# Relative-key products of the diagonal tile: whole-width products against strips of 32 keys

## The chip, the cores and the metric

The kernel runs on one core of one Trainium2 chip. The metric is device time in microseconds (us) of one launch. The engines: PE is TensorE (PEld its weight loads), ACT is ScalarE, DVE is VectorE, POOL is GpSimd, SP only issues DMAs.

## The reference, cut to what matters

Batch 16, sequence 512, model width 128, 16 heads of 8 elements. A layer norm, then attention with relative positions clipped to 20 on either side, then a residual, a second layer norm and a gated feed-forward part of width 384.

```python
idx = jnp.clip(pos[None, :] - pos[:, None], -20, 20) + 20     # (query, key) -> 0..40
rk2, rv2 = rel_k[idx], rel_v[idx]
attn1 = jnp.einsum('bhqd,bhkd->bhqk', q, k)
attn2 = jnp.einsum('bhqd,qkd->bhqk', q, rk2)
attn = softmax((attn1 + attn2) / sqrt(8))
w1 = jnp.einsum('bhqk,bhkd->bhqd', attn, v)
w2 = jnp.einsum('bhqk,qkd->bhqd', attn, rv2)
x = x + (w1 + w2) @ Wo.T + bo
x = x + (silu(ln(x) @ wg.T) * (ln(x) @ wu.T)) @ wd.T
```

What matters here is `attn2`: for a query q only the keys within 20 of it (the band) have a relative row of their own. All keys further below share `rel_k[0]`, all keys further above share `rel_k[40]`.

## The kernel before, in words

There are three stages, one after the other: a projection stage over 16 batches, an attention stage, and an output stage over 16 batches.

**Units and pairs.** The attention stage takes units: one batch and one tile of 128 queries, 64 units in all. Two units of a batch form a pair (32 pairs). Scores are made transposed: keys on the partitions, (head, query) on the columns, in PSUM banks of 512 columns. There are three such banks (`b_s`, NBANK = 3), used in turn. Each pair has 16 chunks, each chunk fills two banks; ACT takes the exponential of each bank (L1111) into `b_p`.

**Chunks of a pair** (`CHUNK`, L602): chunks 0 and 1 are the first unit's diagonal tile (keys and queries of one tile), 2 and 3 its neighbour tile, 4 and 5 another tile; 6 and 7 belong to the second unit's tile at position 0, 8 and 9 are the second unit's diagonal tile, 10 and 11 its tile at position 2, and 12 to 15 the last tile for both units. So there are four diagonal chunks in a pair, 128 in the kernel.

**A diagonal chunk before.** For each of its two banks (n = 0, 1), `scores` (L916) waits for the bank (`wait_bank`), ahead of bank 0 issues the row products of a later unit (`row_pairs_ahead`, L845, two products side by side), then `diagonal_scores` (L909): 8 products of 118 rows by 128 keys on 64 columns (two heads by 32 queries), and then `relative_scores` (L894): 16 products, one for each block of QB = 2 queries, with the 128 keys' weights cut out of the table `z` and 32 columns (16 heads by 2 queries) of the expanded query `qd`. The last of the 16 signals `s_ready` for that bank. Chunk g of the unit has queries 64g to 64g+63 of the tile: bank 0 the first 32 of them, bank 1 the other 32.

The keys carry, as extra rows of the product with K and Q (`DROW` to `ROWS`), the query's product with `rel_k[40] - rel_k[0]`, and K itself carries `rel_k[0]`. On the diagonal tile all keys get the value for "further above", and `z` holds the difference from that.

**Neighbour tiles.** Their relative products (also L904) already use 32 weights: only the strip of 32 keys next to the tile is met. They have 16 columns (8 heads by 2 queries), and all those of a chunk go to one and the same strip. Other products that write strips of 32 partitions are L960, L977, L993, L1010 and L1022; L960, L977, L993 and L1022 go round the four strips in turn.

**The order of the work** is written out by hand: `scores` for each chunk, with other products between the chunks (L1054 to L1084). After chunk 1 stands `guard_transpose` (L1010, three products of the second unit, from pair 1 on; after chunk 3 in pair 0), after chunk 9 `output_transposes` (L1022, 32 products), after chunks 10 and later the value products. A bank with running number x may be written once the exponential of bank x - 3 is done: `wait_bank` waits for `p_ready` of x - 2. A chunk off the diagonal begins with `wait_bank(pair, c, 1)`, ahead of all its products: it needs the exponential of the previous chunk's bank 0. PE holds its instructions in order, with the wait on the first weight load or in front of it.

**ACT's order** (L1136 on): for each chunk the exponential of bank 0, then of bank 1, then what else is due (`guard_copy` after chunk 1, `output_copy` after chunk 7).

Of the kernel before, what the change touches and what calls it, by code (L numbers as in the profile page):

```python
# [8 lines left out]
BF16 = mybir.dt.bfloat16  # L9
I32 = mybir.dt.int32  # L10
ALU = mybir.AluOpType
ACT = mybir.ActivationFunctionType
AX_X, AX_XY = mybir.AxisListType.X, mybir.AxisListType.XY
# [236 lines left out]
def stage_project(nc, m, k, d):  # L250
# [20 lines left out]
    out = k["stored"]  # L271

    z, slot = m.sb("a_z", [P, ZLO_W + ZHI_W]), m.sb("a_slot", [P, PARTS])
    zp, rkj = m.sb("a_zp", [P, ZLO_W + ZHI_W], BF16), m.sb("a_rkj", [P, 2])
    bvb, rvb = m.sb("a_bvb", [P, P]), m.sb("a_rvb", [P, 2, HD])
    wgi, wui, wdi = m.sb("a_wgi", [P, F], I32), m.sb("a_wui", [P, F], I32), m.sb("a_wdi", [P, FC, P], I32)
# [17 lines left out]
    with nc.Block() as block:  # L294
# [212 lines left out]
        def _(dve):  # L507
# [9 lines left out]
            def constants(n):  # L517

                if n == 1:
                    dve.wait_ge(s["late"], 16 * len(late))  # L520
                    chain(nc.vector.tensor_scalar(z[:, 0:ZLO_W], z[:, 0:ZLO_W], rkj[:, 0:1], None, ALU.subtract))
                    chain(nc.vector.tensor_scalar(z[:, ZLO_W:], z[:, ZLO_W:], rkj[:, 1:2], None, ALU.subtract))
                if n in (2, 4, 6):
                    part = n // 2 - 1
                    chain(nc.vector.tensor_copy(zp[:, :], z[:, :]))
                    if part == 0:
                        chain(nc.vector.tensor_scalar(k["z"][:, :], zp[:, :], slot[:, 0:1], None, ALU.mult))
                    else:
                        chain(nc.vector.scalar_tensor_tensor(out=k["z"][:, :], in0=zp[:, :], scalar=slot[:, part:part + 1],
                                                             in1=k["z"][:, :], op0=ALU.mult, op1=ALU.add))  # L530
                if n in (3, 5):
                    chain(nc.vector.tensor_tensor(z[:, :], z[:, :], zp[:, :], ALU.subtract))
                if n == 6:
                    v = k["tvd"][0][:, :].rearrange("p (q d) -> p q d", d=HD)
                    chain(nc.vector.tensor_tensor(k["tvd"][1][:, :].rearrange("p (q d) -> p q d", d=HD), v,
                                                  bc(rvb[:, 1, :], 1, P), ALU.subtract))
                    chain(nc.vector.tensor_tensor(v, v, bc(rvb[:, 0, :], 1, P), ALU.subtract))
                if n == 8:
                    for name, nq, side in (("tvm", CW, 0), ("tvp", CW, 1)):
                        v = k[name][:, :].rearrange("p (q d) -> p q d", d=HD)  # L540
                        chain(nc.vector.tensor_tensor(v, v, bc(rvb[:, side, :], 1, nq), ALU.subtract))
                if n == 9:
                    for side in range(2):
                        chain(nc.vector.tensor_tensor(k["bv2"][:, side, :].rearrange("p (h d) -> p h d", d=HD),
                                                      bvb[:, :].rearrange("p (h d) -> p h d", d=HD),
                                                      bc(rvb[:, side, :], 1, H), ALU.add))
                if n == 10:
                    for half in range(2):
                        chain(nc.vector.tensor_reduce(k["red"][:, :, half, V16 * half:V16 * half + HD],
                                                      k["ident"][:, :].rearrange("p (b j d) -> p b d j", b=WR, d=HD), AX_X, ALU.add))  # L550
                if n == 11:
                    dve.wait_ge(s["zeroed"], 2)
                    for p in range(2):
                        for half in range(2):
                            v = k["vg"][p][:, 0:VW].rearrange("p (s f n c) -> p s f n c", s=2, f=2, c=V32)[:, :, half]
                            nc.vector.memset(v[:, :, :, V16 * half + HD:V16 * half + HDS], 1.0)
# [45 lines left out]
CHUNK = ([(0, 0, g) for g in range(NG)] + [(0, 1, g) for g in range(NG)] + [(0, 2, g) for g in range(NG)]  # L602
         + [(1, 0, g) for g in range(NG)] + [(1, 1, g) for g in range(NG)] + [(1, 2, g) for g in range(NG)]
         + [(None, 3, n) for n in range(CHUNKS - 6 * NG)])
SLICE_DONE = [2 * (max(c for c in range(CHUNKS) if CHUNK[c][1] == pos) + 1) for pos in range(T)]
BESIDE = [c for c in range(CHUNKS) if CHUNK[c][0] is not None and CHUNK[c][1] in ((1,), (0, 2))[CHUNK[c][0]]]

# [25 lines left out]
def stage_attend(nc, m, k, d):  # L633
# [43 lines left out]
        first = n + FIRST + min(n, extra)  # L677
        return [r for r in range(first, first + (2 if n < extra else 1)) if r < HH * U]

    def blocks(t, i, g):  # L680

        half = P // QB // 2
        near = {0: range(half * g, half * (g + 1)), -1: range(REL // QB), 1: range((P - REL) // QB, P // QB)}
        return near[t - i]

    def freed(n):

# [11 lines left out]
    with nc.Block() as block:  # L699
# [134 lines left out]
        def _(pe):  # L834
# [56 lines left out]
                return [(bank(pair, c, hp)[:, (hh - hhs[0]) * PT:(hh - hhs[0] + 1) * PT], K[unit.p][r, hh, t * P:(t + 1) * P],  # L891
                         Q[unit.p][r, hh, hp, q0:q0 + PT], hh == hhs[0]) for hh in hhs]

            def relative_scores(pair, c, unit, only=None):  # L894

                t, g, i = tile_at(pair, CHUNK[c][1]), CHUNK[c][2], unit.i
                heads, nq = (range(H), 32) if t == i else (range(HG * g, HG * g + HG), 64)
                for b in blocks(t, i, g):
                    if only not in (None, QB * b // nq % 2):
                        continue  # L900
                    x0 = (ZLO_0 if t < i else ZLO_W + ZHI_0) + (t - i) * P - QB * b
                    o_ = bank(pair, c, QB * b // nq % 2)[:, :].rearrange("p (h q) -> p h q", q=nq)[:, :, QB * b % nq:QB * b % nq + QB]
                    keys = slice(0, P) if t == i else slice(P - STRIP, P) if t < i else slice(0, STRIP)
                    ins = nc.tensor.matmul(o_[keys], k["z"][0:QROWS, x0 + keys.start:x0 + keys.stop],  # L904
                                           QD[unit.v % 2][0:QROWS, heads[0]:heads[-1] + 1, b * QB:(b + 1) * QB],
                                           start=False, stop=True, skip_group_check=True)
                return ins

            def diagonal_scores(pair, c, unit, n):  # L909

                q0, r = unit.i * P + 64 * CHUNK[c][2] + 32 * n, slice(0, HALF + ROWS)
                for hh in range(HH):
                    nc.tensor.matmul(bank(pair, c, n)[:, hh * 64:(hh + 1) * 64], K[unit.p][r, hh, unit.i * P:(unit.i + 1) * P],  # L913
                                     Q[unit.p][r, hh, :, q0:q0 + 32], start=hh == 0, stop=True, skip_group_check=True)

            def scores(pair, c):  # L916

# [10 lines left out]
                if pos == e:  # L928
                    for n in range(2):
                        wait_bank(pair, c, n)  # L930
                        if n == 0:
                            row_pairs_ahead(pair, c)
                        diagonal_scores(pair, c, unit, n)
                        relative_scores(pair, c, unit, n).then_inc(s["s_ready"], 1)
                    return
                wait_bank(pair, c, 1)
                if c not in BESIDE:
# [152 lines left out]
        def _(act):  # L1090
            def exponentials(pair, c):
                e, pos, g = CHUNK[c]
                if c == 0 and pair:
                    act.wait_ge(s["w_ready"], 2 * pair)
                for n in range(2):
                    act.wait_ge(s["s_ready"], PB2 * pair + 2 * c + n + 1)
                    src = SC[(PB2 * pair + 2 * c + n) % NBANK][:, :]
                    q0 = 0 if e is None else Unit(2 * pair + e).side * P
                    if e is None:
                        src = src.rearrange("p (h q) -> p h q", q=PT)  # L1100
                        out = PR[pos][:, 4 * g + n:4 * g + 4:HP, :]
                    elif pos == e:
                        src = src.rearrange("p (h q) -> p h q", h=H)
                        out = PR[pos][:, :, q0 + 64 * g + 32 * n:q0 + 64 * g + 32 * n + 32]
                    elif c in BESIDE:
                        src = src.rearrange("p (h q) -> p h q", h=HG)
                        out = PR[pos][:, HG * g:HG * (g + 1), q0 + 64 * n:q0 + 64 * (n + 1)]
                    else:
                        src = src.rearrange("p (h q) -> p h q", q=P)
                        out = PR[pos][:, HG * g + n:HG * (g + 1):HP, q0:q0 + P]  # L1110
                    nc.scalar.activation(out, src, ACT.Exp, scale=SCALE).then_inc(s["p_ready"], 1)  # L1111
# [315 lines left out]
def program(nc, d):  # L1427
# [3 lines left out]
    with ExitStack() as keep:  # L1431
# [10 lines left out]
             "x1": [m.sb(f"x1{p}", [P, T, E]) for p in range(2)], "xnT": [m.sb(f"xnT{p}", [P, S]) for p in range(2)],  # L1442
             "aT": m.sb("aT", [P, S]), "out": {n: m.sem("c_s_" + n) for n in OUT_SIGNALS},
             "eps": m.sb("eps", [P, 1]), "root": m.sb("root", [P, 1]), "neg": m.sb("neg", [P, 1]), "one": m.sb("one", [P, 1]),
             "minus": m.sb("minus", [P, P], BF16),
             "stored": [m.sem(f"stored{p}") for p in range(2)], "xo_out": [m.sem(f"xo_out{p}") for p in range(2)],
             "kq_in": [m.sem(f"kq_in{p}") for p in range(2)], "v_in": [m.sem(f"v_in{p}") for p in range(2)],
             "vr": [m.sb(f"vr{p}", [P, S]) for p in range(2)],
# [44 lines left out]
```

## Time and profile before

| | |
|---|---|
| time of three runs, median (lowest to highest) | 1289.37 us (1286.98 to 1291.26) |
| the profiled execution's own time, its span | 1285.89 us, 1284.2 us |
| PE busy | 1211.6 us (94%), 26968 products |
| DVE, ACT, POOL busy | 916.4 us (71%), 735.9 us (57%), 576.4 us (45%) |
| mean granted clock of PE | 0.977 of full |

Busy time is a union: products that run side by side on PE are counted once, while the mean length of one (some 190 ns for small products) is from its start to its end and holds the way through the array. What a product costs in a stream is the distance from its start to the next one's start, and that is read from a timeline. In a timeline a row merges instructions of one kind that follow each other: start, length from the first start to the last end, count.

### The profile page before, as it was taken

What the parts mean: (1) busy time and instruction counts of PE and PEld (TensorE: products, weight loads), DVE (VectorE), ACT (ScalarE), POOL (GpSimd) and SP (SyncE); (2) the same over time, 40 slices, a digit from 0 to 9 for tenths busy, and PEclk for the clock granted to TensorE, in tenths of its full rate; (3) what the DMA queues carried; (4) which work ended last, traced back from release to release, by engine and by line L of the source; (5) the groups of instructions that cost most, each with busy time, mean ns of one, the idle gap of its engine ahead of it and who ended that gap; (6) DMA issues with size and microseconds to landing.
All of it is one profiled execution on the core that took longest, in us unless ns stands there. A gap on an engine that the chain in (4) does not pass through costs nothing. (4 is left out here: it accounts for less than half of the span.)

```text
span 1284.2 us, 60118 instructions
## 1 busy us (share of the span) xinstructions
PE 1211.6 (94%) x26968; PEld 838.5 (65%) x26976; DVE 916.4 (71%) x1751; ACT 735.9 (57%) x1382; POOL 576.4 (45%) x1079
## 2 busy tenths in 40 slices
PE   4788589999999999999999999999999999999998
PEld 3555256676667666666766667677666667767675
DVE  5887777777777777777777777777777776156664
ACT  5787156665666666666666666666666666623332
POOL 5986434453544444544434354544444544022221
PEclk9999579999999999999999999999999999999999
DMA  4576200201111110202020211111110200022321
GB/s 142 185 238 217 66 24 20 59 24 54 37 42 46 32 56 27 63 15 68 10 69 28 59 32 55 46 40 54 36 53 26 69 9 9 8 71 83 90 75 50
DMA packets 101000, 76.51 MB, mean 60 GB/s; under 512 B 12744, under 2 KB 96520, under 8 KB 100744
## 3 DMA queue, kind: packets, MB, share of 16 engines
q1 hardware_dynamic: 100744, 72.67, 19.0%
q8 instruction: 213, 3.49, 1.2%
q14 instruction: 43, 0.35, 0.1%
HBM read 44.86 MB, written 26.21 MB: 55 GB/s over the span
## 5 line engine op out<-in xcount | busy, mean ns | idle before, releaser
L1166 DVE TENSOR_REDUCE b_mx<-b_a 128x1 f32<-128x512 f32 x1024 | 657.7, 685 | 201.2 <-PE b_a L845 197.7
L1111 ACT ACTIVATE b_p<-b_s 128x512 f32<-128x512 f32 x1024 | 569.6, 595 | 379.9 <-PE b_s L904 238.8
L801 POOL TENSOR_TENSOR qd<-q,one 48x512 bf16<-48x512 bf16 x256 | 266.2, 1040 | 479.6 <-PE b_s L904 461.6
L960 PE MATMUL b_pv<-b_p,vg 128*32 128x256 f32 x4096 | 277.0, 384 | 0.2 <-ACT b_p L1111 0.2
L904 PE MATMUL b_s<-qd,z 112*128 112x32 bf16 (+1 forms) x6016 | 248.4, 188 | 0.6 <-issue 0.6
L845 PE MATMUL b_a<-k,q 48*128 48x512 bf16 x1024 | 204.6, 395 | 22.0 <-DVE b_mx L1166 13.2
L904 PEld LDWEIGHTS b_s<-qd,z 112*128 112x128 bf16 (+1 forms) x6016 | 204.6, 98 | 10.6 <-issue 0.7
L866 PE MATMUL b_s<-q,k 54*128 54x64 bf16 (+5 forms) x4096 | 187.6, 206 | 2.7 <-DMA q<-b_mt 1.2
L866 PEld LDWEIGHTS b_s<-q,k 54*128 54x128 bf16 (+1 forms) x4096 | 112.5, 95 | 96.9 <-PE b_s L866 29.5
L960 PEld LDWEIGHTS b_pv<-b_p,vg 128*32 128x32 f32 x4096 | 117.9, 109 | 64.8 <-issue 20.6
L845 PEld LDWEIGHTS b_a<-k,q 48*128 48x128 bf16 x1024 | 51.5, 94 | 87.3 <-ACT b_p L1111 25.9
L913 PE MATMUL b_s<-q,k 118*128 118x64 bf16 x2048 | 105.0, 195 | 0.3 <-issue 0.3
L913 PEld LDWEIGHTS b_s<-q,k 118*128 118x128 bf16 x2048 | 77.5, 99 | 29.8 <-issue 29.7
L977 PEld LDWEIGHTS b_mi<-b_p,tvd 128*32 128x32 f32 x4096 | 76.5, 111 | 13.0 <-issue 2.0
L977 PE MATMUL b_mi<-b_p,tvd 128*32 128x64 f32 x4096 | 83.1, 221 | 1.4 <-issue 1.4
L993 PE MATMUL b_pv<-b_wm,red 128*32 128x128 f32 x2048 | 76.2, 277 | 0.0
L1371 ACT ACTIVATE c_sg<-c_pg 128x512 f32<-128x512 f32 x48 | 28.7, 597 | 60.6 <-PE c_pg L1326 60.6
L1173 DVE TENSOR_TENSOR b_wm<-b_mi,wmask 128x512 f32<-128x512 f32 x64 | 43.9, 687 | 22.6 <-PE b_mi L977 22.6
L219 POOL TENSOR_TENSOR c_std<-c_mv,eps 128x4 f32<-128x4 f32 x15 | 3.0, 199 | 122.4 <-DVE c_mv L212 122.4
L993 PEld LDWEIGHTS b_pv<-b_wm,red 128*32 128x32 f32 x2048 | 51.1, 109 | 6.6
L581 DVE TENSOR_REDUCE a_gr<-a_pr 128x16 f32<-128x640 f32 x64 | 51.3, 816 | 4.8 <-PE a_pr L373 3.4
L1326 PE MATMUL c_pg<-xnT,wg 128*128 128x512 f32 x96 | 50.7, 610 | 0.7 <-ACT xnT L1364 0.7
(144 smaller groups left out, 1224.6 us busy)
## 6 DMA issues: line engine op xcount, KB each, us to landing
x<-in_x SPq DMA_DIRECT2D x24, 256.0 KB, 3.3
scratch_qop<-a_parts SPq DMA_DIRECT2D x16, 384.0 KB, 2.5
scratch_kop<-a_parts SPq DMA_DIRECT2D x16, 384.0 KB, 3.1
k<-scratch_kop SPq DMA_DIRECT2D x32, 192.0 KB
q<-scratch_qop SPq DMA_DIRECT2D x32, 192.0 KB
scratch_v<-a_vr SPq DMA_DIRECT2D x16, 256.0 KB, 3.2
k<-scratch_kop SPq DMA_DIRECT2D x32, 128.0 KB
q<-scratch_qop SPq DMA_DIRECT2D x32, 128.0 KB
```

Of the source, the lines that this page charges most:

```text
L581: nc.vector.tensor_reduce(gr[:, t, :], PR[t % 2][:, :, 0:H * REL].rearrange("p c (h r) -> p h c r", h=H), AX_XY, ALU.max).then_inc(s["relm ...
L801: nc.gpsimd.tensor_tensor(dst, src, one, ALU.mult).then_inc(s["qd_ready"], 1)
L845: nc.tensor.matmul(PA[(HP * n + hp) % NBANK][:, :], Q[p][r, hh, hp, i * P:(i + 1) * P], K[p][r, hh, :], start=True, stop=True).then_inc(s[ ...
L866: ins = nc.tensor.matmul(o_, lhs, rhs, start=first, stop=True, skip_group_check=True)
L904: ins = nc.tensor.matmul(o_[keys], k["z"][0:QROWS, x0 + keys.start:x0 + keys.stop], QD[unit.v % 2][0:QROWS, heads[0]:heads[-1] + 1, b * QB ...
L913: nc.tensor.matmul(bank(pair, c, n)[:, hh * 64:(hh + 1) * 64], K[unit.p][r, hh, unit.i * P:(unit.i + 1) * P], Q[unit.p][r, hh, :, q0:q0 + ...
L960: nc.tensor.matmul(PV[V32 * a:V32 * (a + 1), g * PT:(g + 1) * PT], v[:, side, half, t, 2 * a + g, :], PR[pos][:, 4 * a + 2 * half + g, :], ...
L977: ins = nc.tensor.matmul(MI[r0:r0 + WB * HD, grp * H * WB:(grp + 1) * H * WB], tab[:, q0 * HD:(q0 + WB) * HD], PR[place_of(unit.pair, t)][ ...
L993: ins = nc.tensor.matmul(o_, k["red"][:, b, half, :], w, start=False, stop=True, skip_group_check=True)
L1111: nc.scalar.activation(out, src, ACT.Exp, scale=SCALE).then_inc(s["p_ready"], 1)
L1166: nc.vector.tensor_reduce(MX[unit.v % 2][:, h:h + 1], PA[(HP * n + hp) % NBANK][:, :], AX_X, ALU.max, negate=True).then_inc(s["a_used"], 1)
L1326: nc.tensor.matmul(PG[n][:, :], k["wg"][:, c * P:(c + 1) * P], XNT[at.c % 2][:, :], start=True, stop=True).then_inc(s["gate"], 1)
```

## The change

The diagonal chunks are made otherwise; the rest of the attention stage stays.

- The 128 queries of the tile are four quarters of 32. Chunk 0 of a unit now has quarters 0 and 3, chunk 1 has quarters 1 and 2 (`QUARTERS`), one to a bank. ACT's output slices follow.
- Both banks' products with K and Q come first (16 in all, as many as before), with both bank waits and the row products ahead of them as before; then `diagonal_band` makes the relative products of both banks.
- A relative product now has 32 keys (one strip) instead of 128, the same 32 columns, and only strips that hold part of the band, or lie below it within the table's reach, get one. Chunk 0: 16 blocks of bank 0 on strip 0, 10 on strip 1, and 16 of bank 1 on each of strips 2 and 3: 58. Chunk 1: bank 0 strips 0 and 1 with 16 each and strip 2 with 10, bank 1 strips 1 and 2 with 16 each and strip 3 with 10: 84. Before there were 32 in each chunk.
- Strips further below the band get one constant product for each half of the heads, `diagonal_below`: weights `less` (118 rows by 32), 256 columns. There are four in chunk 0 (bank 1, strips 0 and 1), two in chunk 1 (bank 1, strip 0).
- Signals: in chunk 0 bank 0 is signalled after all 58, bank 1 after the four constant ones. In chunk 1 bank 0 is signalled seven products before the end, bank 1 at the end.
- `less` is built once on DVE in the projection stage, at batch 12: two short reductions, one scaling and one addition.

```diff
@@ projection stage, constants
+                if n == 12:
+                    for half in range(HP):
+                        at_ = HALF * half + DROW
+                        chain(nc.vector.tensor_reduce(ends_[:, half:half + 1], k["ident"][:, at_:at_ + 3], AX_X, ALU.add))
+                    chain(nc.vector.tensor_scalar(ends_[:, :], ends_[:, :], -1.0, None, ALU.mult))
+                    chain(nc.vector.tensor_tensor(k["less"][:, :], ends_[:, 0:1].to_broadcast([P, HALF]),
+                                                  ends_[:, 1:2].to_broadcast([P, HALF]), ALU.add))
@@
+QUARTER = P // 4
+QUARTERS = ((0, 3), (1, 2))
@@ diagonal_scores
-                q0, r = unit.i * P + 64 * CHUNK[c][2] + 32 * n, slice(0, HALF + ROWS)
+                q0, r = unit.i * P + QUARTER * QUARTERS[CHUNK[c][2]][n], slice(0, HALF + ROWS)
@@ new
+            def diagonal_relative(pair, c, unit, n, strip, j):
+                b = QUARTERS[CHUNK[c][2]][n] * QUARTER // QB + j
+                x0, keys = ZLO_W + ZHI_0 - QB * b, slice(STRIP * strip, STRIP * (strip + 1))
+                o_ = bank(pair, c, n)[:, :].rearrange("p (h q) -> p h q", q=QUARTER)[:, :, QB * j:QB * j + QB]
+                return nc.tensor.matmul(o_[keys], k["z"][0:QROWS, x0 + keys.start:x0 + keys.stop],
+                                        QD[unit.v % 2][0:QROWS, :, b * QB:(b + 1) * QB],
+                                        start=False, stop=True, skip_group_check=True)
+            def diagonal_below(pair, c, unit, n, strip, hp):
+                q0, r = unit.i * P + QUARTER * QUARTERS[CHUNK[c][2]][n], slice(0, HALF + ROWS)
+                keys = slice(STRIP * strip, STRIP * (strip + 1))
+                o_ = bank(pair, c, n)[:, :].rearrange("p (hh hp q) -> p hh hp q", hp=HP, q=QUARTER)
+                return nc.tensor.matmul(o_[keys, :, hp, :], k["less"][r, 0:STRIP], Q[unit.p][r, :, hp, q0:q0 + QUARTER],
+                                        start=False, stop=True, skip_group_check=True)
+            def diagonal_band(pair, c, unit):
+                every, late = range(QUARTER // QB), range((QUARTER - REL) // QB, QUARTER // QB)
+                if CHUNK[c][2] == 0:
+                    for j in every:
+                        diagonal_relative(pair, c, unit, 0, 0, j)
+                        if j in late:
+                            diagonal_relative(pair, c, unit, 0, 1, j)
+                        diagonal_relative(pair, c, unit, 1, 2, j)
+                        ins = diagonal_relative(pair, c, unit, 1, 3, j)
+                    ins.then_inc(s["s_ready"], 1)
+                    for hp in range(HP):
+                        for strip in range(2):
+                            ins = diagonal_below(pair, c, unit, 1, strip, hp)
+                    ins.then_inc(s["s_ready"], 1)
+                    return
+                for j in every:
+                    diagonal_relative(pair, c, unit, 0, 0, j)
+                    diagonal_relative(pair, c, unit, 0, 1, j)
+                    diagonal_relative(pair, c, unit, 1, 2, j)
+                    if j in late:
+                        diagonal_relative(pair, c, unit, 1, 3, j)
+                for hp in range(HP):
+                    diagonal_below(pair, c, unit, 1, 0, hp)
+                for j in reversed(every):
+                    if j in late:
+                        ins = diagonal_relative(pair, c, unit, 0, 2, j)
+                    if j == late[0]:
+                        ins.then_inc(s["s_ready"], 1)
+                    ins = diagonal_relative(pair, c, unit, 1, 1, j)
+                ins.then_inc(s["s_ready"], 1)
@@ scores, where pos == e
                         diagonal_scores(pair, c, unit, n)
-                        relative_scores(pair, c, unit, n).then_inc(s["s_ready"], 1)
+                    diagonal_band(pair, c, unit)
```

## Rows read from the trace of the kernel before

**Rows 1.** Windows over the stages: window, length, busy us (instructions) by engine, clock.

```profile
0.00:143.00 143.00, 100.94 (x556) 64.92 (x564) 111.56 (x298) 93.01 (x180) 104.72 (x150) 0.94 0.57 181
155.00:1128.00 973.00, 951.00 (x25503) 664.41 (x25500) 701.21 (x1167) 595.18 (x1121) 430.78 (x879) 0.99 0.14 39
1128.00:1284.20 156.20, 152.11 (x804) 104.64 (x802) 94.67 (x274) 45.64 (x77) 35.94 (x44) 0.99 0.25 74
```

**Rows 2.** Waits by engine and line: waiter, releaser, us in total, times, longest.

```profile
ACT b_p L1111 <- PE b_s L904: 238.8, 294, 6.1
DVE b_mx L1166 <- PE b_a L845: 197.7, 347, 1.6
PEld b_s L866 <- ACT b_p L1111: 27.1, 66, 0.8
```

**Rows 3.** Groups by form: busy us, mean ns of one, idle before.

```profile
L1111 ACT ACTIVATE b_p<-b_s 128x512 f32<-128x512 f32 x1024 | 569.6, 595 | 379.9 <-PE b_s L904 238.8 <-PE b_s L866 125.3
L904 PE MATMUL b_s<-qd,z 112*128 112x32 bf16 x4096 | 168.7, 194 | 0.6 <-issue 0.6
```

**Rows 4.** Timeline of a pair's chunks 0, 1 and the start of 2: start, length, instructions.

```profile
609.75 0.39 PE L845 MATMUL b_a<-k,q 48*128 48x512 bf16 x2
610.08 0.41 PE L913 MATMUL b_s<-q,k 118*128 118x64 bf16 x8
610.32 0.66 PE L904 MATMUL b_s<-qd,z 112*128 112x32 bf16 x16
610.82 0.40 PE L913 MATMUL b_s<-q,k 118*128 118x64 bf16 x8
611.05 0.66 PE L904 MATMUL b_s<-qd,z 112*128 112x32 bf16 x16
611.64 0.39 PE L845 MATMUL b_a<-k,q 48*128 48x512 bf16 x2
...
613.52 0.24 PE L1010 MATMUL b_mi<-b_idb,b_np 128*32 128x128 bf16 x3
613.69 0.29 PE L866 MATMUL b_s<-q,k 51*128 51x64 bf16 x8
```

**Rows 5.** Timeline of strips in turn (L977) with what follows them.

```profile
603.71 0.63 PE L977 MATMUL b_mi<-b_p,tvd 128*32 128x64 f32 x32
...
604.27 0.39 PE L845 MATMUL b_a<-k,q 48*128 48x512 bf16 x2
```

**Rows 6.** Timeline of a chunk with one strip (L904) and ACT behind it.

```profile
622.38 0.38 PE L845 MATMUL b_a<-k,q 48*128 48x512 bf16 x2
622.61 0.29 PE L866 MATMUL b_s<-q,k 54*128 54x64 bf16 x8
622.83 0.39 PE L904 MATMUL b_s<-qd,z 112*32 112x16 bf16 x9
...
623.07 0.17 PE L904 MATMUL b_s<-qd,z 112*32 112x16 bf16 x1
...
623.28 1.08 ACT L1111 ACTIVATE b_p<-b_s 128x512 f32<-128x512 f32 x2 [0.74 <-PE b_s L904]
```

**Rows 7.** Timeline of L866 with 256 columns, between L845 and L960.

```profile
604.50 0.38 PE L866 MATMUL b_s<-q,k 54*128 54x256 bf16 x4
604.81 1.07 PE L960 MATMUL b_pv<-b_p,vg 128*32 128x256 f32 x16
```

**Rows 8.** Timeline around chunks 9 and 10.

```profile
627.40 0.71 PE L1022 MATMUL b_mi<-ident,b_xt 128*32 128x72 f32 x32
628.05 0.29 PE L866 MATMUL b_s<-q,k 51*128 51x64 bf16 x8
...
629.21 0.23 PE L1010 MATMUL b_mi<-b_idb,b_np 128*32 128x128 bf16 x3 [0.17 <-DVE b_xn L1186]
```

**Rows 9.** Timeline in the projection stage: constants on DVE, and PE behind ACT.

```profile
91.57 0.69 ACT L420 ACTIVATE a_parts<-a_pk,bk 128x512 bf16<-128x512 f32 x1
...
92.00 1.60 DVE L544 TENSOR_TENSOR bv<-a_bvb,a_rvb 128x128 f32<-128x128 f32 x2
...
92.32 0.39 PE L380 MATMUL a_pk<-a_parts,minus 128*128 128x512 bf16 x1 [0.43 <-ACT a_parts L420]
98.43 0.78 DVE L549 TENSOR_REDUCE red<-ident 128x32 f32<-128x128 f32 x2
100.03 0.23 DVE L585 COPY a_gd<-a_pq 128x64 f32<-128x64 f32 x1 [0.82 <-PE a_pq L364]
```

More of the change, by code:

```diff
@@ L273, in stage_project @@
     z, slot = m.sb("a_z", [P, ZLO_W + ZHI_W]), m.sb("a_slot", [P, PARTS])
+    ends_ = m.sb("a_ends", [P, HP])
     zp, rkj = m.sb("a_zp", [P, ZLO_W + ZHI_W], BF16), m.sb("a_rkj", [P, 2])
@@ L678, in pairs_beside, with blocks @@
         return [r for r in range(first, first + (2 if n < extra else 1)) if r < HH * U]
[L680 to L684, printed above, removed]
+    def blocks(t, i):
+        return {-1: range(REL // QB), 1: range((P - REL) // QB, P // QB)}[t - i]
     def freed(n):
@@ L892, in far_scores_of_both, with relative_scores @@
                          Q[unit.p][r, hh, hp, q0:q0 + PT], hh == hhs[0]) for hh in hhs]
-            def relative_scores(pair, c, unit, only=None):
+            def relative_scores(pair, c, unit):
                 t, g, i = tile_at(pair, CHUNK[c][1]), CHUNK[c][2], unit.i
[L897 to L900, printed above, removed]
+                heads, nq = range(HG * g, HG * g + HG), 64
+                for b in blocks(t, i):
                     x0 = (ZLO_0 if t < i else ZLO_W + ZHI_0) + (t - i) * P - QB * b
                     o_ = bank(pair, c, QB * b // nq % 2)[:, :].rearrange("p (h q) -> p h q", q=nq)[:, :, QB * b % nq:QB * b % nq + QB]
-                    keys = slice(0, P) if t == i else slice(P - STRIP, P) if t < i else slice(0, STRIP)
+                    keys = slice(P - STRIP, P) if t < i else slice(0, STRIP)
                     ins = nc.tensor.matmul(o_[keys], k["z"][0:QROWS, x0 + keys.start:x0 + keys.stop],
@@ L909, in diagonal_scores @@
             def diagonal_scores(pair, c, unit, n):
-                q0, r = unit.i * P + 64 * CHUNK[c][2] + 32 * n, slice(0, HALF + ROWS)
+                q0, r = unit.i * P + QUARTER * QUARTERS[CHUNK[c][2]][n], slice(0, HALF + ROWS)
                 for hh in range(HH):
                     nc.tensor.matmul(bank(pair, c, n)[:, hh * 64:(hh + 1) * 64], K[unit.p][r, hh, unit.i * P:(unit.i + 1) * P],
-                                     Q[unit.p][r, hh, :, q0:q0 + 32], start=hh == 0, stop=True, skip_group_check=True)
+                                     Q[unit.p][r, hh, :, q0:q0 + QUARTER], start=hh == 0, stop=True, skip_group_check=True)
@@ L1103, in exponentials @@
                         src = src.rearrange("p (h q) -> p h q", h=H)
-                        out = PR[pos][:, :, q0 + 64 * g + 32 * n:q0 + 64 * g + 32 * n + 32]
+                        q0 += QUARTER * QUARTERS[g][n]
+                        out = PR[pos][:, :, q0:q0 + QUARTER]
                     elif c in BESIDE:
@@ L1444, in program @@
              "eps": m.sb("eps", [P, 1]), "root": m.sb("root", [P, 1]), "neg": m.sb("neg", [P, 1]), "one": m.sb("one", [P, 1]),
-             "minus": m.sb("minus", [P, P], BF16),
+             "minus": m.sb("minus", [P, P], BF16), "less": m.sb("less", [P, HALF], BF16),
              "stored": [m.sem(f"stored{p}") for p in range(2)], "xo_out": [m.sem(f"xo_out{p}") for p in range(2)],
```

## The prediction

> **What bounds the kernel now.** First the windows over the stages: the attention stage takes 973 of 1284 us, and PE is busy for 951 of them, ACT for 595, DVE for 701 [rows 1]. Then the waits: ACT waits 239 us for the relative products alone and DVE 198 us for the row products, while PE's largest wait on ACT is 27 us [rows 2]. So PE sets the pace and a nanosecond of PE saved or added in the attention stage is one of the end, unless PE begins to wait. Then the timeline, which gives the distances between starts, the only price that counts in a stream. I work per pair (32 pairs, four diagonal chunks each) and multiply.
>
> **A diagonal chunk before.** From row products to row products it is 611.64 - 609.75 = 1.89 us; the second one ends at 613.52, 1.88 us later [rows 4]. Inside: row products to L913 0.33 us; 8 of L913 in 610.32 - 610.08 = 0.24 us, 30 ns each; 16 of L904 in 610.82 - 610.32 = 0.50 us, 31 ns each [rows 4]. The last L904 starts its busy length less one product's 0.19 us after the first [rows 3, 4], at 611.05 + 0.66 - 0.19 = 611.52, so the step to L845 costs 0.12 us where a further L904 would have cost 0.03. That extra 0.09 us is the price of changing between a full-width product and another shape of the array. The same 0.09 is the difference between L845 to L913 (0.33) and L845 to L866, which keep one shape (622.61 - 622.38 = 0.23) [rows 4, 6].
>
> The Trainium skill, TensorEngine Tiling (Array Packing), Key Properties, says that changing the tiling mode drains TensorE. The step from L904 to L845 just read agrees with it, and the 0.09 us is what enters below.
>
> **The price R of one round of strips.** In the new band loop each block j issues three or four products on different strips, then the next block comes back to the same strips. If strips run beside each other, the loop costs 16 rounds of R, R being the distance between two products of one strip. Rows that bound it:
> - One strip again and again, 16 columns: nine distances in 623.07 - 622.83 = 0.24 us, 27 ns with the first slow one; I take 25 for the later ones, the low end [rows 6].
> - Full width, the same 32 columns taken from the same expanded query: 31 ns [rows 4].
> - Four strips in turn, fp32, 64 columns: 32 products in 604.27 - 603.71 = 0.56 us, less 0.15 for the change of shape and the tail: 31 distances in some 0.42 us, 14 ns each, so 56 ns a round [rows 5]. It shows that strips do run side by side. It is also the fastest sustained pace of products in this trace, so as a pace limit it is the far end.
>
> I take R = 30 ns, near the row with the same number of columns from the same operand (31), because the only 25 has half of them.
>
> The Trainium skill, TensorEngine Tiling, Restrictions, says that column tiling disables the fast weight load. By that a load of 32 weights need not be cheaper than one of 128, and R would be 31, for which the sum below would be 9 us. No row here shows a weight load by itself in the stream.
>
> **Chunk 0 of a unit after.** Row products and 16 of L913 as before: 0.32 + 15 x 0.029 = 0.76 us to the start of the last, change of shape to strips 0.12, so the band starts at 0.88. 16 rounds: 0.48. Then the four constant products: strips 0 and 1 take the first two at once, and the second two wait for them. 256 columns cost 0.11 (half of the 0.31 from the first L866 pair to L960 [rows 7], less the change), so the last starts 0.11 after the band and the next row products 0.11 + 0.09 = 0.20 later. Sum 0.88 + 0.48 + 0.11 + 0.20 = 1.67 us against 1.89: **-0.21** (rounding kept). The relative products themselves go from 0.99 to 0.48; a good half of that is given back by one more change of shape (0.09) and the constant products (0.22).
>
> **Chunk 1 after.** The same 0.88; 16 rounds 0.48; two constant products on one strip, the second holds up the queue 0.11; then 16 rounds again, since strip 1 of bank 1 has 16 products and nothing but strip 2 beside it for ten of them: 0.48. Sum 1.95 against 1.88: **+0.07**. What follows (L1010 or L1022) is a strip product, so the change of shape that it paid before is inside the 1.88 and is gone from the 1.95.
>
> **The wait that the change adds.** In chunk 1 bank 0 used to be signalled 0.73 us (a second bank's products) before the end; now it is signalled seven products before the end, 7R = 0.21. Chunk 2 begins by waiting for that bank's exponential, and the whole of PE's queue stands behind it: row products, value products, everything. From the start of the signalling product: its length 0.17 and 0.04 to ACT's start (623.07 + 0.17 to 623.28) [rows 6], the exponential 0.595 [rows 3], 0.06 from ACT's end to PE (91.57 + 0.69 to 92.32) [rows 9]: 0.87 us. Without the wait chunk 2 would start 0.21 + 0.17 (L1010, 613.52 to 613.69 [rows 4]) = 0.38 after it. **PE stands 0.49 us**, once a pair. ACT is free then (it waits for PE before both exponentials of such a chunk). Two like waits cost nothing: chunk 10's has 0.65 us of L1022 (627.40 to 628.05) before it [rows 8], 0.86 in all against 0.87, and what is left falls into the 0.17 us that PE waits for DVE in that chunk anyway; the second bank of chunk 1 needs chunk 0's bank 0, signalled 0.11 + 0.20 + 0.32 + 0.24 = 0.87 before, just in time. If one of these covers is short by 0.05 us it costs 32 x 0.05 = 1.6 us each.
>
> **DVE's constants** at batch 12: four short linked operations, shorter together than the 1.60 us of L544 or about the 0.78 of L549, and DVE stands idle 0.82 us for PE after those [rows 9]. Cost 0; uncovered at most 0.8 us, once. Moving the queries between banks changes no count of exponentials.
>
> **Sum.** Per pair 2 x (-0.21 + 0.07) + 0.49 = +0.21 us, times 32 = +6.6 us. On the profiled execution's own 1285.9 (span 1284.2 and 1.7 around it) that is 1292.5; that execution is 3.5 below the median of the runs, 1289.4, which gives **1296.0**. By the price of the stall alone (15.7 us) the change would be a gain of 9 without it. Each nanosecond of R moves 2 x 48 - 7 = 89 ns a pair, 2.85 us in all.
>
> **Rivals.**
> - **Fast rounds, a small gain.** If R is 25 as in the strip row, the sum is +6.6 - 5 x 2.85 = -7.6 us: 1281.8. For it: same table, same 32 weights, and that pace hardly varies. Against: half of the columns, and 31 at full width. The break-even is R = 27.7. By the Trainium skill, TensorE: Matmul & The Clock Gate, Wait — 56ns, not 53.3ns?, products start no closer than about 25 ns however few columns they have, 32 included; the strip row [rows 6] agrees and the full-width one [rows 4] lies above it.
> - **Products paced one by one, a clear loss.** Chunks 0 have 58 strip products in 0.48 us, 8 ns each, where no sustained row shows under 14 [rows 5]. If that is a pace limit rather than the 64 columns' own length, each first band costs 58 x 14 = 0.81 us instead of 0.48 (the last 26 of chunk 1 are slower anyway): 4 x 0.33 x 32 = 42 us more, 1338. If a queue filled during L913 hides half, 1317. It decides from 8.3 ns a product on. For it: the distance was never smaller for long. Against: L977's round of four is just what 64 columns of fp32 might take.
> - **Strips that don't run side by side here.** 142 products of 25 ns instead of 64 of 31 in a unit: +1.57 us x 64 = +100 us, 1390. Against it speaks L977 [rows 5]; for it only that those are another type.
> - **No stall**, if something delays chunk 2 anyway: 1280. Nothing in the row order stands there; I put it into the first rival's share.
>
> **How the numbers follow.** The forecast (R 27.5 to 34, stall as worked out) 0.42, its own range 1289 to 1307; fast rounds or no stall 0.40; paced 0.15; serial 0.03. The time is the forecast's, 1296. The range: the fast case reaches 1280, the paced one with half hidden 1317; leaving out the far ends of both, 1279 to 1314. A change under 0.3% (3.9 us) can't be told from none in this kernel. Faster by more: the part of the fast case with R under 26.3, 0.32. Within: the rest of it (0.08) and R from 27.5 to 29 of the forecast (0.14), 0.22. Slower: 0.28 + 0.15 + 0.03 = 0.46.
>
> **What would show it.** In the changed trace: chunk 0 from row products to row products 1.67 us, chunk 1 1.95; the band's first 58 products with a start-to-start length of 0.48; an idle of some 0.5 us on PE before L866 of chunk 2, released by ACT, 31 times; PE busy in the attention stage lower by 9 us or so with its idle time higher by 15; no change in the other two stages. The forecast is wrong if that idle is absent, or if the band takes under 0.42 or over 0.55 us.

## The result

| | median (lowest to highest) | ratio to before, 95% interval | profiled: span, PE busy, PE products |
|---|---|---|---|
| before | 1290.19 us (1286.98 to 1291.26) | | 1284.2, 1211.6, 26968 |
| after | 1378.05 us (1374.82 to 1382.67) | 1.0704 (1.067 to 1.0738) | 1376.9, 1241.7, 32352 |

The change is 88 us slower, where 6.6 were forecast: right in sign, wrong in size by a factor of 13, and far outside the range. The nearest number in the prediction is the rival in which strips don't run side by side (1390), and that is not what happened; that the number lies near is chance.

First the windows over the stages (columns as in rows 1). All of the loss is in the attention stage: 1065 us where there were 973 [rows 1]. PE is busy there for 980 us, 29 more (9 less were forecast), and idle for 85 instead of 22 (15 more were forecast).

```profile
0.00:143.00 143.00, 103.59 (x554) 66.39 (x554) 110.20 (x292) 93.45 (x180) 103.81 (x143) 0.93 0.58 181
155.00:1220.00 1065.00, 980.49 (x30967) 659.34 (x30967) 705.39 (x1174) 584.54 (x1124) 432.29 (x880) 0.98 0.14 37
1220.00:1377.00 157.00, 152.54 (x812) 105.53 (x812) 96.44 (x274) 45.71 (x77) 36.29 (x44) 1.00 0.27 75
```

The waits of the changed kernel (waiter, releaser, us in total, times, longest). The weight loads' largest wait for ACT has grown from 27 us [rows 2] to 48. Much new idle time has no releaser in the profile ("issue": nothing seen ends it). On PE's matmuls of the strips it is 20 us in 33 pieces, where the relative products of before had 0.6 in all [rows 3]. Within the attention stage single pieces reach 1.6 us (the 2.6 lies ahead of the stage):

```profile
PEld b_s L874 <- ACT b_p L1167: 48.4, 107, 0.9
PEld b_a L853 <- issue: 45.8, 134, 2.6
PEld b_s L927 <- issue: 26.1, 37, 1.5
PE b_s L927 <- issue: 20.1, 33, 1.4
```

A pair's chunks 0, 1 and the start of 2 in the timeline, which answers to rows 4 (L853 row products, the former L845; L919 products with K and Q, the former L913; L927 strips; L936 constant products; L1065 the former L1010; L874 the former L866; L1167 the exponential, the former L1111):

```profile
659.04 0.39 PE L853 MATMUL b_a<-k,q 48*128 48x512 bf16 x2
659.37 0.64 PE L919 MATMUL b_s<-q,k 118*128 118x64 bf16 x16
659.94 0.71 PE L927 MATMUL b_s<-qd,z 112*32 112x32 bf16 x54
...
660.57 0.30 PE L936 MATMUL b_s<-q,less 118*32 118x256 bf16 x2
660.81 0.39 PE L853 MATMUL b_a<-k,q 48*128 48x512 bf16 x2
661.13 0.76 PE L919 MATMUL b_s<-q,k 118*128 118x64 bf16 x16
661.82 0.83 PE L927 MATMUL b_s<-qd,z 112*32 112x32 bf16 x61
662.46 0.29 PE L936 MATMUL b_s<-q,less 118*32 118x256 bf16 x1
...
662.95 0.22 PE L1065 MATMUL b_mi<-b_idb,b_np 128*32 128x128 bf16 x1
663.71 0.29 PE L874 MATMUL b_s<-q,k 51*128 51x64 bf16 x8 [0.53 <-ACT b_p L1167]
```

This pair went nearly as forecast. Chunk 0 takes 660.81 - 659.04 = 1.77 us (1.67 forecast, 1.89 before). Chunk 1 takes 2.14 (1.95, 1.88), and PE then waits for ACT: 663.71 - 662.95 = 0.76 us where 0.17 is the step without a wait, so 0.59 (0.49). But two places in its neighbourhood look like this, the first ahead of a chunk far from the diagonal, the second in the middle of eight equal products:

```profile
655.60 0.39 PE L853 MATMUL b_a<-k,q 48*128 48x512 bf16 x2 [0.87 <-issue]
...
678.82 0.23 PE L874 MATMUL b_s<-q,k 51*128 51x64 bf16 x3
680.53 0.26 PE L874 MATMUL b_s<-q,k 51*128 51x64 bf16 x5 [1.48 <-issue]
```

No semaphore stands there. So I numbered all PE records (weight loads, products, waits) in order of time and looked where in that count the long steps from one record to the next lie. In the attention stage 63 steps of more than 0.4 us, 60 us in all, lie at one and the same place of every 256 records; the kernel before has 7 such. The instruction queue on the page moves packets of 16 KB, 255 of them, where the kernel before has 213. Counted as 256 instructions each, 255 packets are 65,280, and PE has 65,382 records; 213 are 54,528, and PE has 54,622. After, then before (packets, MB, share):

```profile
q8 instruction: 255, 4.18, 1.3%
```

```profile
q8 instruction: 213, 3.49, 1.2%
```

So a packet is one block of 256 PE instructions. The new theory: **PE waits for its own instructions**, since a unit's two diagonal chunks now hold 368 in 3.9 us (200 in 3.8 before).

The traces say more on how this goes. Between two boundaries of blocks exactly one packet lands (in 2258 of 2266 blocks of the attention stages of all ten kernels). In the changed kernel it starts 1.1 us (median) after PE has passed the last boundary, takes some 1.2 us, and in the 63 cases has landed 1.4 us (median) before PE goes on. In none of the ten kernels does PE pass a boundary sooner than 2.16 us after the start of that packet. A block that ends in a long step takes 3.8 us in all (median, at least 2.9), 15 ns an instruction, and 1.1 + 1.2 + 1.4 = 3.7 us is just that. So it looks less like a steady pace than like one round trip for each block, which is too long when a block is run through quickly. This can be counted. With the time from one boundary to the last record before the next, so without the step itself, the blocks of the attention stage are, and so many of them end in a step of more than 0.4 us:

| time of a block without the last step | before | after | e8_some | e3_many | all ten kernels |
|---|---|---|---|---|---|
| under 2.8 us | 0 of 0 | 42 of 44 | 0 of 0 | 37 of 44 | 116 of 129 |
| 2.8 to 3.8 us | 3 of 22 | 19 of 67 | 11 of 83 | 41 of 104 | 130 of 542 |
| over 3.8 us | 4 of 180 | 2 of 134 | 5 of 160 | 1 of 134 | 33 of 1595 |

To separate waits that come irregularly from what each pair does, each step between two products was compared with the median of the same place over 28 or 29 pairs; steps that exceed it by more than 0.15 us count as irregular, with the excess. In the last column "the block's place" is within 3 records of the boundary. All kernels of this study by that reading of their traces:

| kernel | time, us | PE products | irregular waits, us a pair | pair without them, us | long steps at the block's place |
|---|---|---|---|---|---|
| before | 1290 | 26968 | 0.21 | 29.83 | 7 |
| after | 1378 | 32352 | 2.34 | 30.49 | 63 |
| e1_early | 1366 | 32344 | 2.17 | 30.32 | 59 |
| e2_full | 1303 | 26968 | 0.41 | 29.97 | 8 |
| e4_few | 1411 | 29016 | 0.14 | 33.57 | 4 |
| e8_some | 1390 | 32088 | 0.63 | 32.47 | 16 |
| e3_many | 1552 | 37208 | 3.19 | 35.02 | 83 |
| e7_sparse | 1290 | 27800 | 0.93 | 29.21 | 21 |
| e5_mix32 | 1297 | 28888 | 0.64 | 29.54 | 18 |
| e6_mix64 | 1288 | 27096 | 0.32 | 29.55 | 7 |

For the change: (2.34 - 0.21) x 32 = **68 us irregular**, (30.49 - 29.83) x 32 = **21 us in every pair**. The 6.6 us forecast stand against the 21; for the 68 the prediction has no term.

### The profile page after: what moved, and what is told of

It reads as the page before. It is cut to its first block and busy times, and to the rows that moved or that the text cites. A ratio compares the mean times of both kernels' runs of the same rounds, so it can differ in the third digit from the quotient of the medians.

```text
span 1376.9 us, 70883 instructions
## 1 busy us (share of the span) xinstructions
PE 1241.7 (90%) x32352; PEld 832.2 (60%) x32352; DVE 922.4 (67%) x1755; ACT 724.0 (53%) x1382; POOL 578.3 (42%) x1079
## 5 line engine op out<-in xcount | busy, mean ns | idle before, releaser
L1167 ACT ACTIVATE b_p<-b_s 128x512 f32<-128x512 f32 x1024 | 556.5, 595 | 479.7 <-PE b_s L927 175.6
L1015 PE MATMUL b_pv<-b_p,vg 128*32 128x256 f32 x4096 | 281.3, 386 | 1.7 <-issue 1.0
L853 PE MATMUL b_a<-k,q 48*128 48x512 bf16 x1024 | 204.9, 395 | 28.6 <-DVE b_mx L1222 13.8
L874 PE MATMUL b_s<-q,k 54*128 54x64 bf16 (+5 forms) x4096 | 189.8, 206 | 23.1 <-ACT b_p L1167 16.7
L874 PEld LDWEIGHTS b_s<-q,k 54*128 54x128 bf16 (+1 forms) x4096 | 113.7, 95 | 121.7 <-ACT b_p L1167 48.4
L927 PE MATMUL b_s<-qd,z 112*32 112x32 bf16 x9088 | 140.0, 202 | 20.4 <-issue 20.1
L927 PEld LDWEIGHTS b_s<-qd,z 112*32 112x32 bf16 x9088 | 118.2, 101 | 32.7 <-issue 26.1
L853 PEld LDWEIGHTS b_a<-k,q 48*128 48x128 bf16 x1024 | 52.3, 94 | 105.5 <-issue 45.8
L919 PEld LDWEIGHTS b_s<-q,k 118*128 118x128 bf16 x2048 | 70.9, 99 | 34.6 <-issue 31.4
L919 PE MATMUL b_s<-q,k 118*128 118x64 bf16 x2048 | 88.9, 195 | 2.0 <-issue 1.4
L910 PE MATMUL b_s<-qd,z 112*32 112x16 bf16 x1920 | 80.2, 176 | 2.0 <-issue 1.8
L910 PEld LDWEIGHTS b_s<-qd,z 112*32 112x32 bf16 x1920 | 60.1, 94 | 12.3 <-issue 2.3
L1236 DVE RECIPROCAL b_rd<-b_mi 128x32 f32<-128x32 f32 x32 | 11.5, 358 | 72.6 <-PE b_mi L1077 72.6
L1229 DVE TENSOR_TENSOR b_wm<-b_mi,wmask 128x512 f32<-128x512 f32 x64 | 44.0, 687 | 22.7 <-PE b_mi L1032 22.6
```

Of the source, the lines that this page charges most:

```text
L853: nc.tensor.matmul(PA[(HP * n + hp) % NBANK][:, :], Q[p][r, hh, hp, i * P:(i + 1) * P], K[p][r, hh, :], start=True, stop=True).then_inc(s[ ...
L874: ins = nc.tensor.matmul(o_, lhs, rhs, start=first, stop=True, skip_group_check=True)
L927: return nc.tensor.matmul(o_[keys], k["z"][0:QROWS, x0 + keys.start:x0 + keys.stop], QD[unit.v % 2][0:QROWS, :, b * QB:(b + 1) * QB], star ...
L1015: nc.tensor.matmul(PV[V32 * a:V32 * (a + 1), g * PT:(g + 1) * PT], v[:, side, half, t, 2 * a + g, :], PR[pos][:, 4 * a + 2 * half + g, :], ...
```

## The experiments

### Signal early; and full width in the new order

`e1_early` has bank 0's 42 strip products of chunk 1 in its first loop (the second loop, cut here, has what is left of bank 1):

```diff
                 for j in every:
                     diagonal_relative(pair, c, unit, 0, 0, j)
-                    diagonal_relative(pair, c, unit, 0, 1, j)
-                    diagonal_relative(pair, c, unit, 1, 2, j)
-                    if j in late:
-                        diagonal_relative(pair, c, unit, 1, 3, j)
+                    diagonal_relative(pair, c, unit, 1, 3 if j in late else 2, j)
+                    if j in late:
+                        diagonal_relative(pair, c, unit, 0, 2, j)
+                    ins = diagonal_relative(pair, c, unit, 0, 1, j)
+                ins.then_inc(s["s_ready"], 1)
```

> The changed kernel with the same 142 strip products and the same constant ones, but in chunk 1 of a unit all products of bank 0 come first, so bank 0 is signalled some 0.4 us earlier. The time to account for is 88 us (1290 to 1378). Theory A (three causes: PE waits for its own instructions some 50 us, the late signal of bank 0 some 18 us, slower rounds some 15 us): the idle of 0.6 us before chunk 2's products shrinks to 0.1 to 0.2, 31 times, so 1362 to 1368; the irregular idle times of 0.4 to 1.6 us stay. Rival B (the late signal is the main cause, the irregular idle follows from it): below 1320. Rival C (strips contend on the array and nothing else): no change, 1378.

Measured 1365.81 us (ratio 1.0571, 1.055 to 1.0592), 12 less than the change. In its timeline the wait of chunk 2 is 623.21 - 622.85 = 0.36 us, less 0.17: 0.19 instead of 0.59.

```profile
622.85 0.22 PE L1064 MATMUL b_mi<-b_idb,b_np 128*32 128x128 bf16 x1
623.21 0.29 PE L874 MATMUL b_s<-q,k 54*128 54x64 bf16 x8
```

So an earlier signal gives 12 us back (0.4 x 31), and the irregular waits stay (2.17 against 2.34 a pair). Theory A had 1362 to 1368. Rival B (below 1320) and rival C (no change) fall.

`e2_full` has the quarters, the order and the slices of the change, but full-width products (cut to the new band):

```diff
+                for n in range(2):
+                    for j in range(QUARTER // QB):
+                        ins = diagonal_relative(pair, c, unit, n, j)     # keys 0..127
+                    ins.then_inc(s["s_ready"], 1)
```

> The changed kernel's quarters, its order (both banks' products with K and Q first) and ACT's new slices, but the relative products full width as before: 32 a chunk, no constant ones. Theory A: instruction count and rounds are as before, bank 0 is signalled half a microsecond before the end, so at most 0.1 us of waiting a pair: 1288 to 1295. A rival that puts the loss on the order, the two bank waits ahead or ACT's slices: above 1310.

Measured 1303.4 us (1.0091, 1.0067 to 1.0116): above the 1288 to 1295 of theory A and below the rival's 1310. Some 0.14 us a pair is regular (4 us); a wait of 0.1 us before chunk 2 is part of it (624.12 - 623.86 = 0.26 us, less 0.16). Another 0.2 a pair, 6 us, is irregular, and why is open. 1378 - 1303 = 75 of the 88 us come with the strips.

```profile
623.86 0.23 PE L1040 MATMUL b_mi<-b_idb,b_np 128*32 128x128 bf16 x3
624.12 0.29 PE L874 MATMUL b_s<-q,k 51*128 51x64 bf16 x8
```

### The number of instructions by itself

Into the kernel before, between the products with K and Q and the relative ones of each diagonal bank, products with zeros as the moving operand are put: 40 of 16 columns in `e3_many`, 8 of 296 in `e4_few`, 20 of 16 in `e8_some` (shown for 40, without the making of the zeros):

```diff
                         diagonal_scores(pair, c, unit, n)
+                        for extra in range(40):
+                            keys = slice(STRIP * (extra % NSTRIP), STRIP * (extra % NSTRIP + 1))
+                            nc.tensor.matmul(bank(pair, c, n)[keys, 0:16], k["z"][:, 0:STRIP], k["zero"][:, 0:16],
+                                             start=False, stop=True, skip_group_check=True)
```

> The kernel before, and in each diagonal bank between the products with K and Q and the relative ones 40 more products on the four strips in turn, 16 columns each, with zeros as the moving operand (they add nothing). By the strip row each strip needs 25 ns a product, so 10 rounds cost 0.25 us of the array, and two changes of shape 0.18: 0.43 x 256 banks = 110 us, the same as in the next kernel. Theory A: 160 more PE instructions a chunk, supplied at no more than one in 13 ns, cost a further 50 to 75 us: 1450 to 1475. Rivals B and C (no limit on instructions): 1400, the same as the next kernel within 5 us.

> As the kernel with 40 added products, but 8 added products of 296 columns (two rounds of four strips, 0.25 us): the same time on the array with a fifth of the added instructions. All theories: 1290 + 110 = 1400 (1390 to 1410); its distance to the kernel with 40 is what the number of instructions costs by itself.

> As the kernel before with 40 added products of 16 columns a diagonal bank, but 20: five rounds, 0.13 us, and the two changes of shape 0.18 to 0.2: 0.32 x 256 = +82 us, 1372. Theory A as a threshold: a chunk has 180 PE instructions in 2.5 us, 14 ns each, just above the supply's 13, so little waiting: 1372 to 1395. If waiting is in proportion to the added instructions instead of a threshold, half of the 140 us that 40 added products cost over few: 1440.

Measured: 40 products 1551.62 us (1.2005, 1.1974 to 1.2036), 8 products 1411.31 (1.0926, 1.0907 to 1.0945), 20 products 1389.97 (1.0779, 1.0757 to 1.0801). The kernel with few lands 11 us above its estimate, that with 20 within theory A's 1372 to 1395 and far from the 1440 of waits in proportion. The 40 cost **140 us** more than the 8; theory A expected 50 to 75, so it has the direction and not the size. In the timeline of the kernel with 40, a product with K and Q in the middle of its row of eight comes after an idle time of 0.80 us with nothing to wait for:

```profile
603.00 0.37 PE L914 MATMUL b_s<-q,k 118*128 118x64 bf16 x7
604.17 0.19 PE L914 MATMUL b_s<-q,k 118*128 118x64 bf16 x1 [0.80 <-issue]
```

The windows over the attention stage (40 first, then 8, then 20) show that the clock differs too:

```profile
155.00:1390.00 1235.00, 1160.96 (x35801) 808.99 (x35799) 704.99 (x1171) 597.04 (x1123) 431.98 (x881) 0.89 0.12 32
```

```profile
155.00:1253.00 1098.00, 1077.45 (x27639) 710.05 (x27639) 705.69 (x1174) 597.50 (x1124) 431.88 (x880) 0.98 0.13 35
```

```profile
155.00:1232.00 1077.00, 1049.24 (x30718) 736.04 (x30719) 704.33 (x1173) 597.46 (x1124) 431.79 (x880) 0.97 0.13 36
```

The granted clock is 0.89 with 40 and 0.98 with 8. By the trace's clock record the kernel with 40 spends 275 us of the stage at 1.2 instead of 2.4 GHz, the one with 8 only 47. How much each part costs can be read in the traces. If a pair is put together from the median step of each place, over the steps at full clock alone, both kernels have the same pair, 33.5 us: at full clock the 40 and the 8 do take the same time on the array. Of what the 40 have above it, irregular waits at full clock are 2.2 us a pair (0.1 with 8), some 67 us. The other 77 or so stand in the stretches at the lower clock, where stops and slower products mix. What brings the clock down was not tested. The stops alone don't explain it: the change has 63 long steps and 36 us at the lower clock, the kernel with 20 only 16 long steps and 63 us.

The kernel with 20 is the other half of the evidence: it has nearly as many PE products as the change (32088 and 32352) and 16 long steps at the block's place against 63. So it is not their number in the kernel but how close they stand: its diagonal chunks hold 180 instructions in 2.53 us (median), 14 ns each, those of the change 160 in 1.77 and 208 in 2.14, 10 to 11.

### Fewer strips, the rest of the change kept

`e7_sparse` leaves out every second block's relative products on the diagonal, so its output lacks them; it serves for the time alone.

```diff
-                every, late = range(QUARTER // QB), range((QUARTER - REL) // QB, QUARTER // QB)
+                every, late = range(0, QUARTER // QB, 2), range((QUARTER - REL) // QB, QUARTER // QB, 2)
```

> The changed kernel with every second block's relative products on the diagonal left out (71 instead of 142 a unit; the output lacks them). Rounds saved: 8 in chunk 0 (0.29 us), 16 in chunk 1 (0.56 us), 54 us over 64 units. Theory A: the instructions left (77 products a unit against 64 before) are supplied in time, so the waits for instructions of some 50 us go too: 1378 - 54 - 50 = 1274 (1265 to 1285). Rival C (array time alone): 1378 - 54 = 1324.

Measured 1290.41 us (1.0012, 0.9993 to 1.0031): 34 below the rival's 1324, 16 above theory A's 1274 and 5 above the end of its range. The irregular waits fall from 2.34 to 0.93 us a pair, 45 us, near the 50 of the theory. What is missing of the saved rounds has two places. The step ahead of chunk 2 grows from 0.74 to 0.92 us (medians), some 6 us in all. And chunk 0 takes 1.46 us (1.76 in the change), but chunk 8 takes 1.79 in both. There PE waits for DVE, which has the masking (L1229) and reductions of 0.68 us each to do:

```profile
599.45 0.68 DVE L1229 TENSOR_TENSOR b_wm<-b_mi,wmask 128x512 f32<-128x512 f32 x1
...
600.05 2.52 DVE L1222 TENSOR_REDUCE b_mx<-b_a 128x1 f32<-128x512 f32 x4
...
600.87 0.39 PE L853 MATMUL b_a<-k,q 48*128 48x512 bf16 x2 [0.26 <-DVE b_mx L1222]
```

In the kernel before DVE was busy through the whole of this chunk, too (the third busy time of the window, 1.89 us of 1.89):

```profile
623.63:625.52 1.89, 1.89 (x50) 1.61 (x52) 1.89 (x4) 1.81 (x4) 0.73 (x4) 1.00 0.03 9
```

So in chunk 8 the gain stayed at 1.89 - 1.79 = 0.10 us, however short PE's own work became.

### Strips only where they pay

Both take the new products in chunk 0 only; chunk 1 is full width in the order of before. In `e5_mix32` chunk 0 is that of the change, in `e6_mix64` it has halves of 64 keys (cut to chunk 0 of the latter):

```diff
+                for j in range(QUARTER // QB):
+                    diagonal_relative(pair, c, unit, 0, range(0, 64), j)
+                    ins = diagonal_relative(pair, c, unit, 1, range(64, 128), j)
+                ins.then_inc(s["s_ready"], 1)
+                for hp in range(HP):
+                    ins = diagonal_below(pair, c, unit, 1, range(0, 64), hp)
+                ins.then_inc(s["s_ready"], 1)
```

> Strips only where they pay: chunk 0 of a unit (quarters 0 and 3) as in the changed kernel, chunk 1 (quarters 1 and 2) with full-width products, each bank's behind its products with K and Q and signalled at once, as before. Chunk 0 was 1.76 us in the changed trace against 1.89: -0.13 x 64 = -8 us; no late signal. Theory A (instruction supply no faster than some 13 ns each): a unit's two chunks have 260 PE instructions in 3.65 us, 14 ns each, so some waits for instructions stay, 0 to 8 us: 1282 to 1292. Rival (loss only from the wait and the second chunk's rounds): 1282.

> As the mixed kernel, but chunk 0 with halves of 64 keys: 16 products on keys 0 to 63 for quarter 0, 16 on keys 64 to 127 for quarter 3, in turn, and two constant products of 64 weights. No more instructions than before. If a 64-wide product costs a half what a 32-wide one costs a strip (31 ns): chunk 0 = 0.88 + 0.50 + 0.11 + 0.20 = 1.69, -0.2 x 64 = -12 us: 1278. If it costs twice that (no fast weight load, 50 ns or more): chunk 0 about 2.0, +7 us: 1297. I expect 1283 with the first the likelier.

Measured: strips of 32 1297.26 us (1.0053, 1.0035 to 1.0072), 5 above the 1292 that theory A allowed; halves of 64 1287.94 (0.9995, 0.9977 to 1.0014), 5 above the 1283 expected. Without irregular waits both have the same pair, 29.54 and 29.55 us, 0.29 less than before (9 us). The one gives it back and more in irregular waits (0.64 a pair), with 1920 more products than before; the other, with 128 more, keeps 0.16 of it in the profile, 5 us, and its timed runs can't be told from before. Halves of 64 keys cost (599.32 - 598.79) / 16 = 33 ns a round, not the 50 of the worse case:

```profile
598.79 0.69 PE L927 MATMUL b_s<-qd,z 112*64 112x32 bf16 x32
599.32 0.39 PE L936 MATMUL b_s<-q,less 118*64 118x256 bf16 x2
599.68 0.39 PE L853 MATMUL b_a<-k,q 48*128 48x512 bf16 x2
```

## Why the prediction was wrong, point by point

- **"A nanosecond of PE saved or added is one of the end, unless PE begins to wait."** The exception was the case, and for something I had no row for. I counted the 84 products that a unit gains only by their time on the array; as 168 instructions more they were costed at nothing. This is the failed step: 68 of the 88 us are irregular waits, and 63 long steps at the ends of blocks hold 60 of them. The page had shown the packets of 16 KB (213 of them). Some 202 of them belong to the attention stage, so there a block of 256 lasted 973 / 202 = 4.8 us in the kernel before; in the diagonal chunks, forecast at 3.62 us for 368 instructions, it would last 2.5. The trace of before alone would have given a doubt and not the price: its quickest blocks took 3.4 us.
- **The rival "paced one by one"** named the right symptom, products too close, with the wrong mechanism: a constant pace on the array or a queue that fills. The array did take them: a first band of 58 went through in 660.52 - 659.94 = 0.58 us, 10 ns each. It stops later, at the next block's end, often in chunks that the change doesn't touch.
- **Strips not side by side:** refuted by the same band, though its 1390 lies near the result.
- **R.** 30 ns was the right price of one strip alone: the second loop of chunk 1 takes 662.95 - 662.46 = 0.49 us for 16 rounds. With three and four strips a round costs 36 ns in chunk 0 (0.58 / 16) and 40 in chunk 1 (661.82 to 662.46). It is a mis-sized term: 6 ns a round in chunk 0 and 10 in half of chunk 1, about 0.1 and 0.16 us. The band took 0.58 us, over the 0.55 that the prediction named as a sign of being wrong. Why four at once are slower than one was not tested.
- **Chunk 0 -0.21, chunk 1 +0.07** came out as -0.12 and +0.26. Besides R, the second bank of chunk 1, called "just in time", waits 0.11 us (L919: 0.76 us for 16 where chunk 0 has 0.64). Chunk 8 was given chunk 0's gain; it got 0.10, held by DVE, whose 1.89 us of work there were in the trace of before.
- **The added wait** was right in place and mechanism, 0.59 us for 0.49: from the signalling product's end (662.88) to ACT's start (663.05) it was 0.17 us, not the strip row's 0.04. Moving the signal gave 12 us back.
- **No cost in the other stages** was right within 1 us.
- The change of shape (L919 to the band) and the constant products (0.11 us between the first two and the last two, 0.20 to the next row products) were as worked out.

The Trainium skill, Runtime: NRT & Kernel Launch, Instruction fetch mechanics, says that an engine's instructions are refilled in blocks of 16 KiB, 256 instructions, by a DMA queue of the sequencer, and calls the crossing of a block's end mostly hidden. The 16 KB packets and the place of the 63 long steps agree with the block; "mostly hidden" holds for the kernel before (7 long steps in 202 blocks) and not for this one (63 in 245). The prediction had not drawn on it.

## What to carry to other kernels

An instruction has a price besides its time on the engine. Here each block of 256 PE instructions came by a packet of its own, at the earliest 2.16 us and in the late cases some 2.6 us before PE could go on, and the packet started about 1 us after the last boundary. Splitting a product into narrower ones that run side by side therefore gained only while a block lasted long enough: under 2.8 us nearly every block ended in a stop, over 3.8 us hardly one, and between them about a quarter. Before splitting, work out how long the densest 256 instructions will last, and look for idle time that no semaphore ends and that returns at a fixed distance in instructions. And where a change makes PE faster in a chunk, look which other engine fills that chunk: its busy time there limits the gain.

## What the runs showed of the hardware that was not expected

- Blocks of 256 PE instructions: one 16 KB packet lands between two boundaries, and in 2266 blocks PE never passed the boundary sooner than 2.16 us after that packet had started. Where the step at the boundary is long, the packet has landed 1.4 us (median) before PE goes on, and the block takes 3.8 us (median).
- Three or four strips in turn: 36 to 40 ns a round, one strip alone 30 to 31, halves of 64 keys 33, with 32 columns each.
- With 83 long steps and 40 small products added to each bank, the granted clock over the stage fell to 0.89 from 0.98. What lowers it is open.
- Open too: what sets off a block's packet and what PE waits for in the 1.4 us after it has landed, and why the full-width kernel in the new order has twice the irregular waits of before with the same number of instructions.
